# Later pairs of a recurrent layer: four of a group's seven Strassen-Winograd sums accumulated in TensorE's banks, two groups multiplied in turn

## The reference

```python
x = L0_attn_x                                   # (8, 512, 512)
xn = _layernorm(x)
q, k, v = xn @ Wq.T + bq, xn @ Wk.T + bk, xn @ Wv.T + bv
phi_q, phi_k = elu(q) + 1, elu(k) + 1
context = phi_q * cumsum(phi_k * v, axis=1) * HEAD_DIM ** -0.5
s = context @ Wo.T + bo
u = fwht(xn * SU_ug) / 64                       # 512 -> 2048 gate and up, silu(gate) * up
h = fwht(silu(u @ W_gate.T * ..) * (u @ W_up.T * ..) * SU_dp) / 64
g = silu(h @ W_down.T * ..)
x = x + s * g
```

## Time and profile before

| | |
|---|---|
| median of 3 runs | 1337.56 us (1337.24 to 1337.63) |
| profiled execution, its own time | 1335.45 us |
| its span, first to last instruction | 1333.6 us |
| TensorE (PE) busy | 1305.5 us, 98%, 6100 matmuls |
| VectorE (DVE) busy | 1011.3 us, 76% |
| ScalarE (ACT) busy | 457.8 us, 34% |
| mean granted TensorE clock | 0.999 |
| pair 1, first product to first product of the down quads | 406.13 to 607.30 us |

### The profile page before, as it was taken

One profiled execution on the slowest core, in us unless ns is written; L12 is line 12 of the kernel. 1 busy time (PEld: TensorE's weight loads), 2 busy tenths in 40 slices (PEclk: granted clock), 3 DMA queues, 4 the chain that ended last, 5 costly groups with the idle time before them and its releaser, 6 DMA issues. The chain is left out here.

```text
span 1333.6 us, 16120 instructions
## 1 busy us (share of the span) xinstructions
PE 1305.5 (98%) x6100; PEld 597.9 (45%) x6100; DVE 1011.3 (76%) x1629; ACT 457.8 (34%) x683; POOL 41.8 (3%) x72
## 2 busy tenths in 40 slices
PE   5999999999999999999999999999999999999998
PEld 3444444444444444444444444444444444444443
DVE  6899999979648997777717998778734998778333
ACT  5945545541123443330113443332112433332000
POOL 0102000001000000000000000000000000000000
PEclk9999999999999999999999999999999999999999
DMA  9624555568264323325244323325244423323240
GB/s 375 246 79 166 198 212 198 180 254 293 94 236 158 127 97 124 127 99 186 97 156 158 127 98 124 126 101 184 95 158 142 143 100 121 127 107 115 95 126 32
DMA packets 47550, 199.39 MB, mean 150 GB/s; under 512 B 5105, under 2 KB 5361, under 8 KB 31985
## 3 DMA queue, kind: packets, MB, share of 16 engines
q1 hardware_dynamic: 41424, 176.87, 36.9%
q0 software_dynamic: 6048, 21.50, 4.4%
HBM read 153.26 MB, written 45.09 MB: 149 GB/s over the span
## 5 line engine op out<-in xcount | busy, mean ns | idle before, releaser
L1455 PE MATMUL bank<-xops,ring 128*128 128x512 f16 x2772 | 601.1, 380 | 3.2 <-DVE work L919 3.1
L1455 PEld LDWEIGHTS bank<-xops,ring 128*128 128x128 f16 x2772 | 269.4, 98 | 334.4 <-DVE work L919 11.3
L919 DVE TENSOR_TENSOR work<-bank,work 128x512 f32<-128x512 f32 x462 | 305.4, 685 | 91.5 <-PE bank L1455 83.9
L1522 PE MATMUL bank<-ring,h_all 128*128 128x512 f16 x1536 | 333.8, 379 | 0.6 <-DMA ring<-scr_d 0.6
L1370 PE MATMUL bank<-xops,ring 128*128 128x512 f16 x1056 | 237.2, 379 | 1.5 <-DVE xops L868 1.5
L1522 PEld LDWEIGHTS bank<-ring,h_all 128*128 128x128 f16 x1536 | 150.0, 98 | 180.9 <-DMA ring<-scr_d 1.1
L1370 PEld LDWEIGHTS bank<-xops,ring 128*128 128x128 f16 x1056 | 102.5, 98 | 140.4 <-issue 28.1
L690 ACT ACTIVATE h_all<-work 128x512 f16<-128x512 f32 x128 | 80.2, 627 | 204.3 <-DVE work L958 204.3
L1189 DVE TENSOR_TENSOR gate_g<-bank,row 128x512 f32<-128x512 f32 x32 | 21.4, 689 | 104.5 <-PE bank L1522 103.9
L740 ACT ACTIVATE gate_g<-gate_g 128x512 f32<-128x512 f32 x32 | 19.9, 630 | 202.9 <-DVE gate_g L1189 202.9
L967 DVE TENSOR_TENSOR h_all<-work,h_all 128x512 f16<-128x512 f32 x128 | 87.4, 685 | 0.4
(11 more groups left out here) (158 smaller groups left out, 835.6 us busy)
## 6 DMA issues: line engine op xcount, KB each, us to landing
ring<-scr_g SPq DMA_DIRECT2D x66, 1024.0 KB, 4.8
ring<-scr_d SPq DMA_DIRECT2D x32, 1024.0 KB, 4.8
scr_g<-ring SPq DMA_DIRECT2D x22, 512.0 KB, 3.5
scr_g<-ring POOLq DMA_DIRECT2D x22, 512.0 KB, 3.5
h_all<-in_ug_t SPq DMA_DIRECT2D x8, 1024.0 KB, 13.9
ring<-scr_f POOLq DMA_DIRECT2D x16, 512.0 KB, 3.7
x_res<-in_x SPq DMA_DIRECT2D x32, 256.0 KB, 3.5
out<-x_res SPq DMA_DIRECT2D x32, 256.0 KB, 6.8
```

Of the source, the lines that this page charges most:

```text
L919: dve.tensor_tensor(tile(g, to), bank[product][:, :], tile(g, other), ALU.add).then_inc(summed, 1)
L1455: mm = pe.matmul(bank[n][:, :], weight_of(slot, s, b, kk), xops[:, kk, xs, c, :], start=(a == 0), stop=(a == 5))
L1522: mm = pe.matmul(bank[D_BANK[t]][:, :], at[:, s, cols], w[:, :, ws, :], start=(a == 0 and b == 0 and n == 0), stop=(a == KB - 1 and b == K ...
```

## The change

In pairs 1 to 3 the sums are made in another place and the products in another order.

- `FACTORS` orders the products so that four of them (P1, P6, P7, P4) run in one bank without clearing it: the bank holds P1, then P1 + P6, then that + P7, then that + P4, which is the complete tile C21. ScalarE copies the bank to SBUF after each of the first three (`copy_sum`). P5 and P3 share a second bank, P2 has a third. Two sets of these three banks alternate by group.
- VectorE adds three times a group (`add`): C11 = copy + P2, C22 = copy + P5, C12 = copy + (P5 + P3). C21 is taken straight from the bank.
- TensorE multiplies two groups in turn (`group_order`): P4 of the group before, P6, P3 of the group before, P2, P7, P1 of the next group, P5.
- In the last group of a pair, the first half of the first down quad (24 matmuls) goes ahead of that group's P4 and P3.
- The order in which ScalarE and VectorE use the tiles follows (`group`, `last_sums`), and so do the waits for banks. The chunks and rows are counted the other way round (`FIRST_CHUNKS`, `ROW_OF`, `CHUNK_OF`, `PLAIN_BANKS`), in pair 0 too, with the same instructions.

```diff
-PRODUCTS = ((A11, B11), (S2, T2), (S3, T3), (S1, T1), (A12, B21), (S4, B22), (A22, T4))
...
+P1, P6, P7, P4, P5, P3, P2 = range(7)
+FACTORS = ((A11, B11), (S2, T2), (S3, T3), (A22, T4), (S1, T1), (S4, B22), (A12, B21))
+CHAIN_BANKS, LEFT_BANKS, RIGHT_BANKS = (0, 1), (2, 3), (4, 5)
...
-PLAIN_BANKS = (1, 2, 3, 0)
+C11, C22, C21, C12 = range(4)
+PLAIN_BANKS = (0, 1, 2, 3)
...
+def group_order(g):
+
+    if g == 0:
+        return [(0, P1), (0, P2), (0, P6), (0, P5), (0, P7), (1, P1)]
+    head = [(g - 1, P4), (g, P6), (g - 1, P3), (g, P2), (g, P7)]
+    if g < GROUPS - 1:
+        return head + [(g + 1, P1), (g, P5)]
+    return head + [(g, P5), (g, P4), (g, P3)]
...
-                    sp.wait_ge(product_done, 7 * nth(p, n) + 7)
+                    sp.wait_ge(product_done, products_to(p, n, P3))
...
+            def copy_sum(p, g, n):
+
+                j = (C11, C12, C22)[n]
+                act.wait_ge(product_done, products_to(p, g, (P1, P6, P7)[n]))
+                wait_free(act, p, g, j)
+                act.activation(tile(g, j), chain_bank(g)[:, :], ACT.Copy).then_inc(copied, 1)
...
             def group(p, g):
+                if g == 0:
+                    copy_sum(p, g, 0)
+                elif kind_of(g - 1) != IS_UP:
+                    take(p, g - 1, C22)
+                copy_sum(p, g, 1)
+                if g and kind_of(g - 1) == IS_UP:
+                    take(p, g - 1, C22)
                 if g:
-                    take(p, g - 1, 2)
-                copy_p1(p, g)
+                    take(p, g - 1, C21)
+                copy_sum(p, g, 2)
+                if g + 1 < GROUPS:
+                    copy_sum(p, g + 1, 0)
                 if g:
-                    take(p, g - 1, 3)
-                take(p, g, 0)
-                take(p, g, 1)
+                    take(p, g - 1, C12)
+                take(p, g, C11)
...
+            def add(p, g, j):
+
+                at, m = ((right_bank(g), P2), (left_bank(g), P5), None, (left_bank(g), P3))[j]
+                dve.wait_ge(product_done, products_to(p, g, m))
+                dve.wait_ge(copied, 3 * nth(p, g) + (1, 3, 0, 2)[j])
+                dve.tensor_tensor(tile(g, j), at[:, :], tile(g, j), ALU.add).then_inc(summed, 1)
...
             def group(p, g):
                 if g:
-                    add(p, g - 1, 6)
-                    use(p, g - 1, 2)
-                    hidden_low(p, g - 1, 1)
-                add(p, g, 0)
+                    use(p, g - 1, C22)
+                    hidden_low(p, g - 1, C11)
+                    use(p, g - 1, C21)
+                    hidden_low(p, g - 1, C22)
+                    add(p, g - 1, C12)
+                add(p, g, C11)
                 if g:
-                    use(p, g - 1, 3)
-                    hidden_low(p, g - 1, 2)
-                add(p, g, 1)
+                    use(p, g - 1, C12)
+                    hidden_low(p, g - 1, C21)
+                add(p, g, C22)
                 if g:
-                    hidden_low(p, g - 1, 3)
-                add(p, g, 2)
-                add(p, g, 3)
-                add(p, g, 4)
-                use(p, g, 0)
-                add(p, g, 5)
-                use(p, g, 1)
-                hidden_low(p, g, 0)
+                    hidden_low(p, g - 1, C12)
+                use(p, g, C11)
...
+            def wait_bank(p, g, m):
+
+                if m == P1:
+                    if g >= 2:
+                        wait_taken(pe, p, g - 2, C21)
...
+                elif m in (P6, P7, P4):
+                    pe.wait_ge(copied, 3 * nth(p, g) + (P6, P7, P4).index(m) + 1)
...
+                elif m == P3:
+                    pe.wait_ge(summed, 3 * nth(p, g) + 2)
...
+                if g + 1 == GROUPS:
+                    down_part(2 * p, 0, (0, 1))
+                    product(p, g, P4)
+                    product(p, g, P3)
+                    down_part(2 * p, 0, (2, 3))
```

More of the change, by code:

```diff
@@ L768, in _ @@
                     group(p, g)
-                take(p, GROUPS - 1, 2)
-                take(p, GROUPS - 1, 3)
+                for j in (C22, C21, C12):
+                    take(p, GROUPS - 1, j)
                 if p < PAIRS - 1:
@@ L955, in hidden @@
                 src = tile_in(dve, p, g, j)
-                if p == 0:
+                if p == 0 or j == C21:
                     wait_free(dve, p, g, j)
@@ L1446, in group @@
[L1446 to L1457, removed]
+            def wait_bank(p, g, m):
+                if m == P1:
+                    if g >= 2:
+                        wait_taken(pe, p, g - 2, C21)
+                    else:
+                        pe.wait_ge(z_ready, 8 * p - 4 + (2, 3)[g])
+                elif m in (P6, P7, P4):
+                    pe.wait_ge(copied, 3 * nth(p, g) + (P6, P7, P4).index(m) + 1)
+                elif m == P5:
+                    if g >= 2:
+                        pe.wait_ge(summed, 3 * nth(p, g - 2) + 3)
+                    elif g == 1:
+                        pe.wait_ge(o_read, 8 * p - 4 + 1)
+                    else:
+                        pe.wait_ge(z_ready, 8 * p - 4 + 4)
+                elif m == P3:
+                    pe.wait_ge(summed, 3 * nth(p, g) + 2)
+                elif g >= 2:
+                    pe.wait_ge(summed, 3 * nth(p, g - 2) + 1)
+                else:
+                    pe.wait_ge(o_read, 8 * p - 4 + (2, 3)[g])
@@ new lines, in product @@
+            def product(p, g, m):
+                slot = slot_of(p, g)
+                if m == P1:
+                    pe.wait_ge(slot_loaded[slot], 16 * loads_into(p, g))
+                    if g == 0:
+                        pe.wait_ge(x_ready, 2 * p + 2)
+                wait_bank(p, g, m)
+                to = chain_bank(g) if m in (P1, P6, P7, P4) else right_bank(g) if m == P2 else left_bank(g)
+                b, c = FACTORS[m]
+                terms = [(kk, s, xs) for kk in range(2) for s, xs in ((HI, HI), (HI, LO), (LO, HI))]
+                for a, (kk, s, xs) in enumerate(terms):
+                    mm = pe.matmul(to[:, :], weight_of(slot, s, b, kk), xops[:, kk, xs, c, :],
+                                   start=(a == 0 and m in (P1, P2, P5)), stop=(a == 5),
+                                   skip_group_check=True)
+                mm.then_inc(product_done, 1)
@@ L1509, in down_quad @@
                 pe.wait_ge(slot_loaded[slot], 16 * loads)
[L1510 to L1520, removed]
[L1521 to L1525 removed]
+                for b in range(KB):
+                    k = KB * QUADS[a] + b
+                    i, r = k % 8, k // 8
+                    if cc == 0:
+                        pe.wait_ge(h_ready, 32 * p + 4 * i + 4)
+                    w, at = quad(slot)[:, :, b, :, :], h[:, i, 2 * r + cc, :, :]
+                    for t in ts:
+                        if a == 0 and b == 0:
+                            wait_down_bank(c, t)
+                        cols = slice(t * P, (t + 1) * P)
+                        for n, (s, ws) in enumerate(((HI, HI), (HI, LO), (LO, HI))):
+                            mm = pe.matmul(bank[D_BANK[t]][:, :], at[:, s, cols], w[:, :, ws, :],
+                                           start=(a == 0 and b == 0 and n == 0),
+                                           stop=(a == KB - 1 and b == KB - 1 and n == 2))
+                if ts[-1] == TB - 1:
+                    mm.then_inc(quad_done, 1)
+            def down_quad(c, a):
+                for ts in ((0, 1), (2, 3)) if a == 0 else ((0, 1, 2, 3),):
+                    down_part(c, a, ts)
             def out_product(c, t):
```

112 lines of the change are left out of this document (56 added, 56 removed).

## The result

The change is slower: 1349.3 us, median of 4 runs (1348.0 to 1351.3), against 1337.4 us before (1336.5 to 1337.6). The ratio is 1.0092, 95% interval 1.0074 to 1.0109: 12 us. The forecast was 1345.2 us, the range stated with it 1339.0 to 1351.5.

A forecast was written before the change was run, and what follows sets the result against it. TensorE, busy 98% of the span, bounds the kernel; faster sums return at most 5.2 us. Group waits +1.0 and pair ends +6.6 give +7.6 on 1335.45 us, 1343.05; plus 2.1 to the median, 1345.2 us, range 1339.0 to 1351.5.

The forecast's parts named there:

- rival A: Pair ends: the forecast's waits, and the clock falls at both; +13.2 us, 1350.8 us; chance 0.12.
- Part 1: Four sums a group leave VectorE: 181 us less there, 79 us more on ScalarE; at most 5.2 us back.
- Part 2: Chained bank makes TensorE wait among the groups: 2.07 us a pair, 6.2 in place of 5.2, so +1.0 us.
- (a): Group 1, once a pair: ScalarE's table load, Exp and Relu delay copies; TensorE waits 0.42 and 0.11 us.
- (b): V tiles, twice a pair: TensorE waits 0.28 us, 8.05 us of chain against six products, 7.77.
- (c): Q tiles, twice a pair: P3 waits 0.49 us for the sum for C22, 4.37 us against three products, 3.88.
- rival B: Gate and up groups: ScalarE late by 0.1 us in each of 48; +4.8 us, 1350.0 us; chance 0.10.
- Part 3: Ends of pairs 1 and 2: P4 and P3 behind 24 down matmuls start VectorE's chain 3.3 us later; +6.6 us.
- The clock: Pair ends: about 3.5 us of idle time might lower TensorE's clock, 2.8 us a time; not in the forecast sum.
- Part 4: Weight loads issued later and pair 0 renumbered: zero; bounds 1 us either way for pair 0.
- C: Waits among the groups all go, only the pair ends' stay: +1.4 us, 1339.0 us; chance 0.13.
- D: VectorE reaches the pair's end with time in hand, next tokens not late: -5.2 us, 1332.4 us; chance 0.06.

The follow-up runs named there:

- Run 7: Changed kernel with three edits together: P4 and P3 ahead of the down quad, C22 sum earlier, function table loaded ahead of each pair: 1330.8 us, ratio 0.9960.
- run 4: Changed kernel, but in attention groups VectorE makes the sum for C22 ahead of the last tile of the group before: 1346.2 us.
- run 5: Changed kernel with a one-column Exp on ScalarE ahead of each pair, loading the function table there: 1346.5 us, one execution.
- Run 6: Changed kernel with SyncE's load of the next tokens issued ahead of that of the out weights: 1353.3 us, one execution.
- run 2: Kernel before, with only the last group's last two products moved behind the first 24 down matmuls: 1352.6 us, ratio 1.0114.
- run 1: Changed kernel, but the last group's P4 and P3 stay ahead of all 48 matmuls of the first down quad: 1336.9 us, ratio 1.0000.
- run 3: Changed kernel with 12 down matmuls instead of 24 ahead of the last group's P4 and P3: 1341.4 us, ratio 1.0036.

## Why the prediction was right, and where its size was off

The direction and the place were right: slower, because TensorE waits at the ends of pairs 1 and 2. That mechanism holds, and it makes up most of the loss. What came on top of it, a lowered clock behind both waits, is rival A, to which the prediction gave 0.12. The measured +12.0 us lies between the forecast, +7.6, and rival A, +13.2. The forecast's own range, 1342 to 1348.5, didn't hold it.

**What bounds the kernel.** Right. The sums could give back 5.2 us by pair 1, 5.6 us with pair 2 counted. Run 7 has it: without a wait among the groups and at the pair ends it is 5.8 us faster than before. By the rows of before, 5.6 us and the 0.7 us of the pair ends, it would be 6.3.

**Part 1** was right: 264 sums less gave nothing by themselves. VectorE's busy time fell by 158 us and not by 181, to 853 us and not near 830: I took 0.685 us for a sum, but instructions of this size that follow each other start 0.60 us apart (648.73, 649.33, 649.93 in VectorE's timeline at the end of pair 1), and 264 x 0.60 is 158.

**Part 2, the three loops.** (a) 0.42 and 0.11 us forecast, 0.39 and 0.11 measured; (b) 0.28 forecast, 0.36 measured; (c) 0.49 and 0.48. The sum, +1.0 us, measured +1.1. Runs 4 and 5 take the cause of each away and the wait goes with it. "Zero" for the gate and up groups was right, so rival B falls. (b) was 0.08 us too small; which hand-over it is I didn't follow up.

**Part 3, the pair ends**, is the term that was mis-sized: 6.6 us forecast, 7.7 measured. 0.27 us a pair are the low part, at 8.34 us and not 8.07, and 0.21 of them have this cause: I let `hidden` start 0.58 us behind the sum, as independent instructions do, but it reads what the sum writes and started 0.79 us behind it. The rest is in pair 2, where VectorE waited 0.48 and 1.57 us for the tokens, against 0.36 and 0.55 us before; GpSimd gave back 0.48 us of these 1.14 (VectorE's wait for it was 3.46 us, before 3.94). The longer wait, in the changed kernel and before:

```profile
941.39 2.47 DVE L871 BATCH_NORM_STATS2 stats<-work 128x6 f32<-128x512 f32 x4 [1.57 <-DMA work<-in_x]
```

```profile
929.30 2.47 DVE L829 BATCH_NORM_STATS2 stats<-work 128x6 f32<-128x512 f32 x4 [0.55 <-DMA work<-in_x]
```

That is the unknown for which I had bounds of 0 and 1.9 us a pair, and took 0. Run 6 speaks against the nearness of the out weights' load as its cause. It does go with the move: in pair 2 the two waits together were 1.9 to 2.5 us in all five kernels that have 24 matmuls ahead, and 0.6 to 0.9 us in the four others. Why, stays open.

**The clock** is the step that failed. I gave the fall 0.12 because 3.5 us of idle time seemed nearer to the 2.00 that did nothing than to 14.64. It came at both pair ends. The price of 2.8 us by the earlier trace rows was that of a longer fall than this: there the first 26 of the 32 transposes stood about 0.21 us apart, over 5.4 us, and the last ones 0.11. In the profiled execution of the changed kernel the slow stretches were shorter and cost 1.7 us each; in runs 4 and 6 they cost 2.6 to 2.8. That rival A's value came within 1.2 us of the measured one is in part luck: its clock term was 2.2 us too high and its waits 1.2 us too low. With both as measured, 1.1 + 7.7 + 3.4 = 12.2 us stands against 12.0. At the pair ends the Trainium skill's rule (TensorE: Matmul & The Clock Gate, section "Why this matters for your kernels"), no idle gaps above about 3 us, would have decided rightly. The trace agrees with it there: 1.4 and 1.67 us of idle time left the clock alone, 3.65 us and more lowered it at all ten pair ends of five kernels. In pair 0 it doesn't: idle times of 2.26 to 2.48 us, below the rule's 3, were followed by the lower level too, as part 4 shows.

**Part 4.** The renumbering of pair 0 cost nothing, though the changed profile is 1.6 us late there. Its wait at 72 us was followed by a lowered clock too, and so was that of the kernel before's own pair 0 in run 2. The wait of both, with the 24 matmuls that follow it; first the changed kernel, then run 2, then run 6, which has the changed kernel's pair 0:

```profile
72.72 1.12 PE L1434 MATMUL bank<-h_all,hada 128*128 128x512 f32 x2 [2.41 <-DVE h_all L1139]
73.68 7.03 PE L1401 MATMUL bank<-xops,ring 128*128 128x512 f16 x24
```

```profile
72.69 1.67 PE L1403 MATMUL bank<-h_all,hada 128*128 128x512 f32 x2 [2.38 <-DVE h_all L1107]
74.15 6.53 PE L1370 MATMUL bank<-xops,ring 128*128 128x512 f16 x24
```

```profile
72.77 1.12 PE L1434 MATMUL bank<-h_all,hada 128*128 128x512 f32 x2 [2.47 <-DVE h_all L1139]
73.73 5.34 PE L1401 MATMUL bank<-xops,ring 128*128 128x512 f16 x24
```

Run 6 idled as long as the other two and kept its clock: 5.34 us. Over the nine profiled executions the clock fell at this place in six (the kernel changed, runs 1, 2, 3, 4 and 7, idle time 2.26 to 2.48 us) and stayed up in three (the kernel before with 2.00 us, run 5 with 1.74, run 6 with 2.47). Where it fell pair 1 begins at 407.33 to 408.67 us, where it didn't at 406.13 to 406.42, with either version of pair 0 on both sides. So those 1.7 us (7.03 for 5.34) belong to no version of the code.

Rivals C and D fall with the waits that were measured.

## What to carry to other kernels

When work is moved to give one short chain more room, look up what else waits for its result: here two products went behind 24 matmuls to cover waits that run 1 shows there was no need to cover, and a chain on VectorE 38 us long, at whose end TensorE already waited 0.3 us, began that much later. A place where the busiest engine waits even a quarter of a microsecond has no slack at all, and a delay ahead of it counts in full: here 3.57 us in pair 1 made 3.5 us of wait. Count a wait of some microseconds on TensorE together with the clock that it can lower, not by itself.

## What the runs showed of the hardware

- Idle time of TensorE and its clock, in nine profiled executions: it never fell after idle times up to 2.19 us. Of nine from 2.26 to 2.83 us it fell after six and not after 2.39, 2.47 and 2.83 us (the first and the last of these at 22 us of runs 2 and 6, behind the first transposes); so the length doesn't decide alone, and 2.41 and 2.47 us at the same place of the same code went different ways. After 3.65 us and more it fell ten times of ten. A fall at a pair end cost 1.4 to 2.8 us of 48 matmuls (11.93 to 13.33 us for 10.52). I had not expected the same code to show both.
- Adding four products into one bank, with ScalarE reading it between them, cost nothing that shows: in run 4 the 269 matmuls from 422.01 us take 58.34 us, 0.216 us each, as before.
- An Exp or a Relu read from a bank took 0.77 us, from SBUF 0.80 us.
- GpSimd began the power of the variances 1.2 to 3.8 us behind VectorE's last step on them at the ends of pairs 1 and 2, in the kernels of this study. The cause stays open.
